# Attention value sums through an SBUF copy, rotation ahead of the pieces, and the first four query chunks in four PSUM banks

## What is computed

```
q_nope, q_pe = split(x @ wq)                     # 128 + 64 columns per head
ckv, k_pe = split(x @ wkv_a);  ckv = rmsnorm(ckv) * kv_norm_scale
k_nope, v = split(ckv @ wkv_b)
qs = [q_nope, rope(q_pe)];  ks = [k_nope, rope(k_pe)]
scores = where(causal, qs @ ks.T / sqrt(192), min)
out = softmax(scores) @ v;   return out @ wo
```

## Time and profile before

| what | us |
|---|---|
| median of 3 runs (range) | 1399.17 (1397.67 to 1401.56) |
| the profiled execution | 1404.18 |
| its span, first to last instruction | 1402.4 |
| busy in the span: PE, DVE, ACT, POOL | 1188.5, 789.7, 697.6, 956.0 |
| first attention phase, about | 493 to 865 |
| second attention phase, about | 908 to 1285 |

### The profile page before, as it was taken

The page is one execution under the profiler, slowest core; times in us unless marked ns, Lnnn a source line. Parts: engine busy times, 40 slices in busy tenths (PEclk is TensorE's granted clock), DMA queues, the critical chain, the costliest instruction groups (busy, mean ns, idle before and its releaser), DMA issues. The chain is left out here.

```text
span 1402.4 us, 18855 instructions
## 1 busy us (share of the span) xinstructions
PE 1188.5 (85%) x5570; PEld 877.9 (63%) x5625; DVE 789.7 (56%) x1712; ACT 697.6 (50%) x1325; POOL 956.0 (68%) x700
## 2 busy tenths in 40 slices
PE   6983688999995469999999997779999999998797
PEld 5873555555553336767767675746667766677686
DVE  4468722222221756666766672847666676663566
ACT  3220123233321227677776785237777777785242
POOL 2024868888884648778887776648777887777454
PEclk9985889999998569999999999969999999999899
DMA  9449235555555300000000000000000000002001
GB/s 325 135 136 240 90 64 79 81 81 82 79 80 92 118 15 4 5 8 9 8 6 3 1 1 13 8 8 8 1 8 8 9 8 1 1 1 66 1 16 46
DMA packets 66512, 68.22 MB, mean 49 GB/s; under 512 B 15072, under 2 KB 59680, under 8 KB 66304
## 3 DMA queue, kind: packets, MB, share of 16 engines
q1 hardware_dynamic: 48336, 43.36, 10.5%
q0 software_dynamic: 15168, 20.72, 9.5%
q10 hardware_dynamic: 2928, 3.15, 0.7%
HBM read 46.10 MB, written 21.10 MB: 48 GB/s over the span
## 5 line engine op out<-in xcount | busy, mean ns | idle before, releaser
L1529 POOL TENSOR_TENSOR att_prob_lo<-att_prob,att_prob_hi 128x1024 fp32r<-128x1024 f32 (+1 forms) x160 | 347.1, 2174 | 85.7 <-ACT att_prob_hi L1457 85.7
L1358 PE MATMUL all_bank<-att_q_hl,sequence_k_hl 128*128 128x512 f32 (+1 forms) x960 | 257.1, 378 | 0.0
L1381 PE MATMUL all_bank<-att_prob_hi,sequence_v_hl 128*128 128x512 f32 (+1 forms) x640 | 190.4, 379 | 16.8 <-ACT late_oT L1469 15.3
L1450 ACT ACTIVATE att_prob<-all_bank 128x1024 f32<-128x1024 f32 (+1 forms) x160 | 150.0, 938 | 86.0 <-PE all_bank L1364 81.8
L1358 PEld LDWEIGHTS all_bank<-att_q_hl,sequence_k_hl 128*128 128x128 f32 x960 | 172.1, 191 | 28.3
L1341 PE MATMUL all_bank<-sequence_k_hl,att_q_hl 128*128 128x512 f32 (+3 forms) x384 | 170.1, 448 | 8.1 <-DVE att_peak L1577 6.0
L1457 ACT CAST att_prob_hi<-att_prob 128x1024 fp32r<-128x1024 f32 (+1 forms) x160 | 154.3, 964 | 5.1
L1328 PE MATMUL all_bank<-sequence_x_hl,sequence_w_hl 128*128 128x512 f32 x384 | 115.1, 438 | 48.1 <-DVE all_xT L1567 40.5
L917 PE MATMUL all_bank<-early_w_gu,moe_xgT 128*128 x316 | 148.8, 554 | 3.6 <-issue 2.5
L882 POOL DMA_INDIRECT sums<-moe_y,early_slot_far x79 | 125.4, 1588 | 36.3 <-issue 17.8
L1381 PEld LDWEIGHTS all_bank<-att_prob_hi,sequence_v_hl 128*128 128x128 f32 x640 | 112.7, 189 | 41.0 <-issue 22.1
(11 more groups left out here) (245 smaller groups left out, 2175.3 us busy)
## 6 DMA issues: line engine op xcount, KB each, us to landing
sequence_w_raw<-wqk_rows SPq DMA_DIRECT2D x16, 256.0 KB, 2.7
early_w_gu<-in_gate SPq DMA_DIRECT2D x16, 224.0 KB, 5.9
early_w_gu<-in_up SPq DMA_DIRECT2D x16, 224.0 KB, 6.0
early_w_down<-in_down SPq DMA_DIRECT2D x1, 3584.0 KB, 21.4
sums<-early_zero SPq DMA_DIRECT2D x18, 128.0 KB, 3.7
all_xT<-in_xT SPq DMA_DIRECT2D x4, 512.0 KB, 7.7
all_x_tok<-in_x SPq DMA_DIRECT2D x1, 2048.0 KB, 16.4
x_rows<-all_x_tok SPq DMA_DIRECT2D x4, 512.0 KB, 3.0
```

The lines of the kernel that those rows point to most:

```text
L1358: nc.tensor.matmul(ps, k_hl[:, ks, j * P:(j + 1) * P], q_hl[n % 2][:, qs, :, i * BW + q0:(i + 1) * BW], start=g == 0, stop=False)
L1381: mm = nc.tensor.matmul(out, v_hl[:, vs, j, :], part[:, u % 3, half * WIDE:half * WIDE + 2 * w].rearrange("p (h m) -> p h m", h=2), start= ...
L1450: nc.scalar.activation(prob[:, u % 2, 0:w], s_ps[u % 2][:, 0:w], ACT.Exp, scale=SCALE).then_inc(prob_sb, 1)
L1529: nc.gpsimd.tensor_tensor(prob_lo[:, u % 3, 0:w], prob[:, u % 2, 0:w], prob_hi[:, u % 3, 0:w].bitcast(F32), ALU.subtract).then_inc(lo_sb, 1)
```

## The change

The value sums are copied whole, 128x512, into a new SBUF tile `both`; that copy alone releases bank 4 (`free_sb`). The four 64x256 copies follow as `lay`, from `both`, and the wait for the inversions moves to them. DVE takes `aside`'s list as it stands, the rotation first. The four chunks of pair 0 go to banks 0 to 3 without a wait between them; the first scores, which take over those banks, wait for all four rotations instead.

```diff
+        both = m.sb("both", [P, WIDE])
+        clear_sb, free_sb = m.sem("clear_sb"), m.sem("free_sb")
-        pv_ps, q_ps = bank[:, 4, :], bank[:, 5, :]
+        pv_ps = bank[:, 4, :]
+        q_bank = lambda n, k: bank[:, 5, :] if n else bank[:, k, :]
...
-                    if n * QC + k:
+                    if n:
                         pe.wait_ge(sin_sb, n * QC + k)
...
                         if jj == 0 and e >= 1:
-                            pe.wait_ge(sums_sb, e)
+                            pe.wait_ge(free_sb, e)
...
+                pe.wait_ge(sin_sb, QC)
                 scores(0, 0)
...
                 def sums(n, i):
+                    act.wait_ge(pv_mm, n * NG + last_of[i] + 1)
+                    nc.scalar.copy(both[:], pv_ps).then_inc(free_sb, 1)
+
+                def lay(n, i):
                     e = n * NB + i
-                    act.wait_ge(pv_mm, n * NG + last_of[i] + 1)
+                    act.wait_ge(free_sb, e + 1)
                     if e >= 2:
                         act.wait_ge(rden_sb, 2 * (e - 1))
                     for h in range(2):
...
-                        nc.scalar.copy(own, pv_ps[LORA:P, cols])
-                        done = nc.scalar.copy(oT[half, n, i * BW:(i + 1) * BW], pv_ps[0:LORA, cols])
+                        nc.scalar.copy(own, both[LORA:P, cols])
+                        done = nc.scalar.copy(oT[half, n, i * BW:(i + 1) * BW], both[0:LORA, cols])
                     done.then_inc(sums_sb, 1)
...
                         sums(n, last_of.index(x))
+                        lay(n, last_of.index(x))
...
-                    items = aside(n, x)
-                    if items and items[0][0] == "query":
-                        items[0:2] = items[1::-1]
-                    for item in items:
+                    for item in aside(n, x):
                         beside(item)
```

More of the change, by code:

```diff
@@ L1299, in phase_attention @@
              "rden_sb", "o_sb"))
-        clear_sb = m.sem("clear_sb")
+        both = m.sb("both", [P, WIDE])
+        clear_sb, free_sb = m.sem("clear_sb"), m.sem("free_sb")
         s_ps = [bank[:, 2 * s:2 * s + 2, :].rearrange("p a n -> p (a n)") for s in range(2)]
-        pv_ps, q_ps = bank[:, 4, :], bank[:, 5, :]
+        pv_ps = bank[:, 4, :]
+        q_bank = lambda n, k: bank[:, 5, :] if n else bank[:, k, :]
         piece_ps = [bank[:, n, :] for n in (6, 7)]
@@ L1327, in query @@
                         for kc in range(KC):
-                            mm = nc.tensor.matmul(q_ps, w_hl[:, ws, kc, h * P:(h + 1) * P],
+                            mm = nc.tensor.matmul(q_bank(n, k), w_hl[:, ws, kc, h * P:(h + 1) * P],
                                                   x_hl[:, xs, kc, c * WIDE:(c + 1) * WIDE],
@@ L1563, in rope @@
                     for i, o in ((LORA + 32, LORA), (LORA, LORA + 32)):
-                        nc.vector.tensor_tensor(swapped[o:o + 32, c % 2], q_ps[i:i + 32], sin[i:i + 32, cols], ALU.mult)
+                        nc.vector.tensor_tensor(swapped[o:o + 32, c % 2], q_bank(n, k)[i:i + 32], sin[i:i + 32, cols], ALU.mult)
                     if c >= 2:
                         dve.wait_ge(q_lo_sb, c - 1)
-                    nc.vector.tensor_tensor(raw[:, c % 2], q_ps, cos[:, cols], ALU.mult).then_inc(sin_sb, 1)
+                    nc.vector.tensor_tensor(raw[:, c % 2], q_bank(n, k), cos[:, cols], ALU.mult).then_inc(sin_sb, 1)
                 def peaks(n, y):
```

## The result

The changed kernel takes 1349.50 us (median of 4 runs, 1346.89 to 1351.65) where the kernel before takes 1400.37 (4 runs, the three shown above among them). The ratio is 0.9638, 95% interval [0.9614, 0.9662]. The profiled execution took 1350.13 us with a span of 1348.3, so 54.05 us less than the profiled execution of before, where the sum of the prediction says 57.

The account below looks back on a forecast made before the run. PE's stream was taken to set the pace, other engines mattering only where PE waits. 34 + 17 - 3 - 1 + 10 = 57 us off the profiled 1404.18 gave 1347.2, less 5.0 to the median: 1342 us, range 1330 to 1364.

Parts of the forecast that it names:

- rotation ahead: Middle pairs: PE's waits for DVE's rotation ahead of query chunks go, a gain of 34 us (27.1 to 38.4).
- value sums: Attention: PE's 32 waits for the last copy of a block nearly all go, a gain of 17 us.
- last pairs: Last pair of each sequence: without queries as cover, ACT's added copy costs 3 us for both sequences.
- phase ends: End of each attention phase: the last block's extra copy stands alone on the path, 1 us lost.
- openings: Both openings: four chunks in four banks bring the first peaks earlier, a gain of 10 us (6 to 13.4).
- seven pairs of each sequence, three waits in each: Middle pairs: the count behind the 42 query waits, 27.1 us as recorded, that the rotation's move should remove.
- rival 3: Steps with rotation ahead of pieces: peaks become the wait and take all the rotation's gain, 1376 us; chance 0.06.
- the upper bound: Rotation's high end: 27.1 us recorded plus 0.27 us of stream refill for each of 42 waits, 38.4 us.
- Nearly all go: Value sums: of PE's 32 waits, 15.3 us with mean 0.48 and longest 1.1, nearly all vanish.
- Rival 1: Middle pairs: the wait moves to POOL's low parts in every pair, 21 us, giving 1363; chance 0.17.
- Rival 2: Openings: PE's clock rises later after four chunks and an idle, up to 5.2 us each, 1352 us; chance 0.08.
- the profiled execution is 5.0 us above the median: Last step of the sum: 5.0 us taken off 1347.2 to give the forecast median of 1342 us.

Follow-up runs that it names:

- e1: The kernel before with only the rotation moved ahead of the piece, value sums and banks as before; 1360.48 us, ratio 0.9700.
- e4: The changed kernel with the wait for the inverted sums again ahead of the whole copy; 1351.66 us, ratio 0.9645.
- e10: The changed kernel with each sequence's last block laid out straight from its bank and the last pair's first three blocks laid out by VectorE; 1341.89 us.
- e9: The changed kernel with only each sequence's very last block laid out straight from its bank, without the whole copy; 1345.12 us.
- e6: The changed kernel with 26 unread TensorE matmuls more per sequence, 16 in the opening and 10 behind the last value sums; 1345.21 us.
- e8: The changed kernel with blocks laid out one step later, the last straight from its bank, plus the extra matmuls of e6; 1348.45 us.
- e11: e10 with filler matmuls behind the last value sums, 24 in the first sequence, 10 in the second, none in the openings; 1342.33 us.
- e3: The kernel before with only the first four query chunks of each sequence given four banks; 1390.70 us, ratio 0.9927.
- e5: The changed kernel with the value sums put back to four copies straight from the bank; 1353.35 us, ratio 0.9660.

## Why the prediction was right

Direction and size were right; several terms of the sum were not, and made up for each other, so that the total for the attention came out so close is in part luck. The steps, with what the trace has for each (before against changed, both sequences):

| term | predicted | in the trace |
|---|---|---|
| rotation ahead | 34 | 33.3: from the chunk of step 0 to that of step 3, on average 16.54 to 13.79 us in six pairs of each sequence, 12 x 2.75; pair 0 only 0.3 in all |
| value sums | 17 | 15.8: from step 3's chunk to the next pair's, 27.27 to 26.15 in six pairs of each sequence (13.4), and in the seventh to the last pair's first values, 28.63 to 27.41 (2.4) |
| last pairs | -3 | -0.4: from there to the end of the last values, 29.26 to 29.48 |
| phase ends | -1 | -1.6: gaps 6.05 and 2.67 to 6.84 and 3.45 |
| openings | 10 | 9.7: 32.75 + 34.91 - 28.74 - 29.22 |
| attention | 57 | 56.8 |
| other stages | 0 | -2.7: outputs 1.0 and 2.9 longer, the stages ahead of the attention 1.2 shorter, MoE 0.1 |
| whole | 57 | 54 |

**Rotation.** The step "seven pairs of each sequence, three waits in each" was wrong in one of the seven. In pair 0 the wait changed its name, from the query's to that of the third piece's peak (0.70 at 525.30), and the steps kept their length. That is rival 3, in the one pair where a step has three pieces of its own. The other twelve pairs gained 2.75 us each where I had 34 / 14 = 2.43, since the whole of the stream's refill came back: as the upper bound had it (38.4 x 12 / 14 = 32.9). The two errors cancelled.

**Value sums.** "Nearly all go" is what the waits show, 15.3 to 2.6 us. But the step from the wait to its cause failed: the profile names ACT's copy as the releaser, and I took the copy's length as the cause. e1 shows that half of the 15.8 us, 7.9, comes with the rotation alone (7.2 of the 13.4 and 0.7 of the 2.4), through the inversions on DVE; the copy adds the other 7.9, of which e4 puts 3.0 to the moved wait.

**Last pairs.** Of the 3 us charged 0.4 were paid. The last pair did become longer, by 0.22 us in each sequence. The wait of step 9 grew, from 0.75 to 1.53 us, as the step said, and 1.31 stands behind ACT in another step; but waits of 0.29 and 1.13 (at 834.42 and 844.93) went beside the 0.90 of the earlier trace rows, and they nearly pay for both. The tail is 1.0 us shorter because it begins in the seventh pair, whose value sums gained 1.22. The 17 had counted the last pairs' waits as gained and the -3 took them back, so the two terms are best read together: 14 predicted, 15.4 in the trace. e10 shows that ACT is the limit in the last pair (29.48 to 27.25 us there). Rival 1 is confined to this place: no low part is waited for in any other pair, though e4 shows that 0.3 us more on ACT is enough to bring it into the middle pairs, as a delay too short to be listed.

**Phase ends.** The extra copy is alone on the path, as said: 0.79 and 0.78 us with its start, and e9 takes them away again.

**Openings.** From the first rotation to the first peak 10.74 us (495.07 to 505.81) where I had 11.4, so the first peaks come 5.5 and 5.7 us earlier. The openings gained 4.0 and 5.7. Over all kernels here the four-bank openings take 27.3 to 30.6 us and the others 31.2 to 35.9. Rival 2 was right about the clock of the first opening, 0.50 and then 0.74 where the earlier trace rows has 0.95, and the 1.5 us missing there is its price: from the first peak to the end 14.96 us instead of 13.44. In the second opening the clock was low before too, and that stretch is unchanged (15.40 and 15.44). So rival 2 happened in one opening of two, at 1.5 us where it allowed 5.2 for each; e6's fillers, which raise the clock of the first 6 us behind the peak only, do not win it back.

**What the sum left out.** It ended with the attention. The largest loss, 2.9 us, came in the second output stage, whose first 20 us had a granted clock of 0.85 against 0.93 before. That this is the clock's price is shown by e6, e8 and e11, with 1.00 there and 37.9 to 38.0 us, and by PE's busy time, 31.87 us for 225 matmuls against 28.99 in e6. It does not follow any one part of the change: e1 and e3 took 38.0 and 38.1, e5 without the copy 40.7. The last step, "the profiled execution is 5.0 us above the median", took a property of one execution for one of the kernel: the profiled execution after is 0.6 us above its median. Of the 7.5 us between 1342 and 1349.5 that step made 4.4, and the sum's 57 against 54 made the other 3.

## What to carry to other kernels

When a wait is put down to an engine, look at what that instruction itself waited for just before; a fix one engine further back can take both waits, and two fixes for one chain don't add up (7.9 and 11.1 us alone, 15.8 together). A step that is put first for the common case can cost its gain in the odd iteration that has one more piece of work, so price the first and the last iteration by their own rows. Judge small gains by lengths inside a stage that repeat to hundredths, not by totals in which other stages vary by 1 to 3 us, and compare those other stages only at the same granted clock.

## What the hardware showed unexpectedly

VectorE's copy from SBUF to SBUF takes 0.29 us alone and up to about the length of a GpSimd operation longer when one is running. DVE's timeline in the last pair of e10:

```profile
808.78 0.29 DVE L1612 COPY att_den<-att_both 64x256 f32<-64x256 f32 x1
809.08 0.28 DVE L1613 COPY late_oT<-att_both 64x256 f32<-64x256 f32 x1
809.38 0.29 DVE L1612 COPY att_den<-att_both 64x256 f32<-64x256 f32 x1
809.69 2.39 DVE L1613 COPY late_oT<-att_both 64x256 f32<-64x256 f32 x1
```

And POOL's timeline of e10 at the same time:

```profile
809.43 2.50 POOL L1545 TENSOR_TENSOR att_prob_lo<-att_prob,att_prob_hi 128x1024 fp32r<-128x1024 f32 x1 [0.96 <-ACT att_prob_hi L1460]
```

The first three copies take 0.28 to 0.29 us. The fourth takes 2.39 and ends at 812.08, just behind the low part, which ends at 811.93. The Trainium skill, "SBUF — State Buffer", section "SBUF: two separate sides", says that GpSimd and certain VectorE operations, an fp32 copy from SBUF to SBUF among them, hold a shared pair of ports as an exclusive lock for a whole instruction, so that the later one waits; these rows agree. For e10 it cost little, since DVE had nothing else to do there. In a middle pair the same copies would stand among rotations and peaks, and ACT, whose copies from `both` took 0.40 us whether or not POOL was at work beside them (232 and 24 copies of the changed kernel), is probably the better place; that was not tried.
